# A written-out engine order drawn up anew for the last third of a four-layer kernel, with the residual rows fetched by pairs of tiles

## What is computed

```python
x = x + tanh(g_xattn[0]) * additive_attention(layernorm(x), ctx)            # phase A
x = x + tanh(g_ffn[0]) * quantized_gated_ffn(layernorm(x))                  # phase B, its down projection in C

# third layer, 16 heads of 32 channels, 64 keys per batch
qh = layernorm(x) @ Wq.T + bq
attn = softmax(where(mask, qh @ kh.T / sqrt(32), -inf))
x = x + tanh(g_xattn[1]) * ((attn @ vh) @ Wo.T + bo)

# fourth layer: bit_linear 512 -> 2048, depthwise convolution of 3 taps along the tokens, silu, bit_linear
def bit_linear(x, w):            # 8-bit activations per token, ternary weights
    return act_quant(x) @ weight_quant(w).T
h = bit_linear(layernorm(x), w1)
h = silu(conv_w[0] * h[t-1] + conv_w[1] * h[t] + conv_w[2] * h[t+1] + conv_b)
x = x + tanh(g_ffn[1]) * bit_linear(h, w2)
```

## Time and profile before

| quantity | value |
|---|---|
| median of three runs | 2092.08 us |
| time of the profiled execution | 2092.43 us |
| its span, first to last instruction | 2090.3 us |
| TensorE busy (share of the span) | 1651.5 us (79%) |
| VectorE busy | 1729.7 us (83%) |
| ScalarE busy | 1476.9 us (71%) |
| GpSimd busy | 626.2 us (30%) |
| mean of what DMA moved | 69 GB/s |

### The profile page before, as it was taken

The page is one execution under the profiler, slowest core; times in us unless marked ns, Lnnn a source line. Parts: engine busy times, 40 slices in busy tenths (PEclk is TensorE's granted clock), DMA queues, the critical chain, the costliest instruction groups (busy, mean ns, idle before and its releaser), DMA issues.

```text
span 2090.3 us, 24728 instructions
## 1 busy us (share of the span) xinstructions
PE 1651.5 (79%) x9617; PEld 748.7 (36%) x9686; DVE 1729.7 (83%) x2574; ACT 1476.9 (71%) x1109; POOL 626.2 (30%) x487
## 2 busy tenths in 40 slices
PE   6868866796569767955979678988888888888886
PEld 3212211221113112312434356656666543334332
DVE  6889998999999988885877657877787669999994
ACT  4899999999999999993537434444444466666650
POOL 0000000000000000000612345655555447677773
PEclk9999999999999999997999899999999999999997
DMA  5001100020000100003957423323322112111111
GB/s 189 1 21 46 41 6 1 21 81 11 1 1 16 56 1 1 8 3 112 331 201 263 157 78 94 99 71 101 102 84 86 41 36 66 61 51 51 61 41 61
DMA packets 104551, 143.68 MB, mean 69 GB/s; under 512 B 8046, under 2 KB 61422, under 8 KB 104050
## 3 DMA queue, kind: packets, MB, share of 16 engines
q1 hardware_dynamic: 104434, 142.09, 20.4%
HBM read 91.74 MB, written 50.33 MB: 68 GB/s over the span
## 4 chain that ended last, share of the span: by engine, by line
ACT 41%; PE 32%; DVE 17%; issue 4%; POOL 3%; DMA 2%; SPq 0%; DVEq 0%; POOLq 0%; ACTq 0%
ACT unit L514 37%; PE psum L1598 5%; PE psum L1632 5%; PE psum L1584 4%; DVE hmax_parts L1404 3%; PE psum L1009 3%; PE psum L1015 2%; POOL hidden L1776 2%; DVE psum L1395 2%; DVE unit L423 2%; PE psum L1608 2%; PE psum L1625 2%; DMA xblk<-xnT_scratch 2%; PE psum L1617 1%; DVE hidden_q L1431 1%
## 5 line engine op out<-in xcount | busy, mean ns | idle before, releaser
L514 ACT ACTIVATE unit<-unit 128x4096 f32<-128x4096 f32 x244 | 857.5, 3617 | 0.5 <-DVE unit L423 0.3
L423 DVE TENSOR_SCALAR unit<-feat_proj,text_proj 128x1024 f32<-128x1024 f32 x976 | 667.5, 747 | 67.0 <-PE psum L639 65.3
L639 PE MATMUL psum<-unit,w_pad 128*32 128x512 f32 x3904 | 474.5, 604 | 234.1 <-ACT unit L514 234.1
L639 PEld LDWEIGHTS psum<-unit,w_pad 128*32 128x32 f32 x3904 | 102.6, 109 | 556.8 <-ACT unit L514 398.6
L680 POOL TENSOR_SCALAR red<-red 128x8 f32<-128x8 f32 x4 | 2.0, 510 | 531.5 <-DVE red L321 531.5
L1759 POOL TENSOR_TENSOR h<-h,arow 128x512 f32<-128x512 f32 x104 | 122.3, 1187 | 87.1 <-ACT h L1540 87.1
L1656 PE MATMUL psum<-xq_block,w_q 128*128 128x512 bf16 x489 | 128.1, 399 | 24.5 <-ACT hidden L1563 23.2
L1690 PE MATMUL psum<-w_q,hidden_q 128*128 128x512 fp8e4 x512 | 122.3, 394 | 25.9 <-DVE hidden_q L1431 25.5
L1776 POOL TENSOR_TENSOR hidden<-hidden,srow 128x2048 f32<-128x2048 f32 x32 | 130.5, 4078 | 37.2 <-DVE hidden_q L1431 23.4
L1598 PE MATMUL psum<-xnT_c,wq_sb 128*128 128x256 f32 x512 | 119.9, 388 | 11.0 <-ACT xnT_c L1497 11.0
L547 PE MATMUL psum<-xnT,W_sb 128*128 128x512 f32 x256 | 125.2, 617 | 2.1 <-ACT xnT L465 2.1
(11 more groups left out here) (241 smaller groups left out, 2864.9 us busy)
## 6 DMA issues: line engine op xcount, KB each, us to landing
h_scratch<-h SPq DMA_DIRECT2D x44, 512.0 KB, 3.9
hin<-h_scratch SPq DMA_DIRECT2D x32, 704.0 KB, 5.4
xin<-in_x SPq DMA_DIRECT2D x8, 1024.0 KB, 6.7
tern_in<-in_w1T SPq DMA_DIRECT2D x16, 512.0 KB, 5.6
tern_in<-in_w2T SPq DMA_DIRECT2D x16, 512.0 KB, 5.5
x<-in_x SPq DMA_DIRECT2D x32, 256.0 KB, 2.8
x_scratch<-x SPq DMA_DIRECT2D x32, 256.0 KB, 2.1
x3in<-x_scratch SPq DMA_DIRECT2D x31, 256.0 KB, 2.9
```

Of the source, the lines that this page charges most:

```text
L423: ins = ve.tensor_scalar(units[:, n % 3, k, :], FP[:, bi % 2, k, :], TP[:, k, n:n + 1], None, ALU.add)
L514: ac.activation(units[:, n % 3], units[:, n % 3], ACT.Tanh).then_inc(unit_tanh, 1)
L639: mm = te.matmul(psum[k * TG:(k + 1) * TG, 3 + 2 * grp + half, :], w_pad[:, k, TG - 1 - tt:2 * TG - 1 - tt], units[:, n % 3, k, half * BAN ...
```

## The change

The tables of slots are new in both halves. The period of a group goes from 256 to 226 slots, that of a block from 350 to 363. A tile is further from its first to its last step: the last step of group 0 (XQ) had slot 1084 and has 1276. One convolution chunk moves from TensorE's taps to VectorE's, and one from the multiplication by ScalarE and GpSimd to VectorE's. The residual rows are fetched once per group (512 KB in one transfer, into both tiles of the ring) instead of once per tile, at a slot behind the start of the group and no longer 74 slots ahead of it; the fetch of `hin` moves from HQ1's slots to HQ2's. The arithmetic of each tile stays as it was.

```diff
-    N1, N2, OFF2 = 256, 350, 4330
+    N1, N2, OFF2 = 226, 363, 4140
...
-    DOWN = (38, 102)
+    DOWN = (350, 416)
...
-    X2LOAD = (-74, -50)
-    GP_MID, VE_MID = (0, 1, 2, 4, 5, 6, 7, 9, 10, 11, 12, 13, 15), (3, 8, 14)
-    PE_TAPS, VE_TAPS = (1, 6, 11), (0, 2, 3, 4, 5, 7, 8, 9, 10, 12, 13, 14, 15)
+    X2LOAD = (324,)
+    GP_MID, VE_MID = (0, 1, 2, 3, 5, 6, 8, 9, 10, 12, 13, 15), (4, 7, 11, 14)
+    PE_TAPS, VE_TAPS = (2, 9), (0, 1, 3, 4, 5, 6, 7, 8, 10, 11, 12, 13, 14, 15)
...
             for g, i, t in at1(q, X1):
-                A.wait_ge(x2_loaded[g % GR], 16 * TPG * (g // GR + 1))
+                A.wait_ge(x2_loaded[g % GR], 16 * (g // GR + 1))
...
-        def load_x(t):
-            S.wait_ge(ln3_done, t - X2R + 1)
-            S.wait_ge(x3_stored[t // TPG % GR], 16 * TPG * (t // X2R))
-            sp.dma_start(x2[:, t % X2R, :], x[t * P:(t + 1) * P, :]).then_inc(x2_loaded[t // TPG % GR], 16)
+        def load_x(g):
+            S.wait_ge(ln3_done, TPG * (g + 1 - GR))
+            S.wait_ge(x3_stored[g % GR], 16 * TPG * (g // GR))
+            rows = x[g * GRP:(g + 1) * GRP, :].rearrange("(i p) d -> p i d", p=P)
+            sp.dma_start(x2[:, g % GR * TPG:(g % GR + 1) * TPG, :], rows).then_inc(x2_loaded[g % GR], 16)
 
         def attention(q):
-            for g, i, t in at1(q, HQ1):
+            for g, i, t in at1(q, X2LOAD):
+                load_x(g)
+            for g, i, t in at1(q, HQ2):
                 if t + 2 < NT:
                     load_tile(t + 2)
-            for g, i, t in at1(q, X2LOAD):
-                load_x(t)
...
-        for q in range(X2LOAD[0], QEND):
+        for q in range(min(0, X2LOAD[0]), QEND):
```

More of the change, by code:

```diff
@@ L1235, in flamingo @@
-    PTAP = (239, 316, 416)
-    SILU = (268, 274, 281, 300, 320, 328, 345, 356, 371, 431, 443, 448, 466, 478, 519, 531)
-    AROWMM = (0,)
[L1238 to L1250, removed]
+    N1, N2, OFF2 = 226, 363, 4140
+    LEN1, LEN2 = 1283, 1020
@@ new lines, in flamingo @@
+    SHIFT = (0, 128)
+    HQ1 = (154, 264)
+    HQ2 = (174, 276)
+    DOWN = (350, 416)
+    DSC = (374, 470)
+    X1 = (388, 402)
+    X2ADD = (396, 490)
+    ST2 = (442, 510)
+    ROOT2 = (466, 518)
+    LN2 = (482, 532)
+    BO = (502, 540)
+    TURN2 = (560, 636)
+    XNT = (574, 644)
+    QMM = (668, 740)
+    QT = (700, 772)
+    SCORE = (792, 824)
+    MADD = (802, 840)
+    SMAX = (814, 858)
+    SUB = (826, 870)
+    EXP = (844, 888)
+    SSUM = (874, 900)
+    SREC = (890, 914)
+    NRM = (900, 924)
@@ new lines, in flamingo @@
+    TURNP = (924, 994)
+    PT = (940, 1006)
+    PV = (1002, 1110)
+    OT = (1020, 1122)
+    WO = (1058, 1156)
+    X3 = (1094, 1192)
+    ST3 = (1108, 1200)
+    ROOT3 = (1118, 1208)
+    LN3 = (1134, 1218)
+    AMAX = (1142, 1224)
+    Q3 = (1152, 1230)
+    Y3 = (1158, 1238)
+    TURN3 = (1186, 1270)
+    XQ = (1192, 1276)
+    X2LOAD = (324,)
+    GP_MID, VE_MID = (0, 1, 2, 3, 5, 6, 8, 9, 10, 12, 13, 15), (4, 7, 11, 14)
+    PE_TAPS, VE_TAPS = (2, 9), (0, 1, 3, 4, 5, 6, 7, 8, 10, 11, 12, 13, 14, 15)
@@ new lines, in flamingo @@
+    W1 = (197, 206, 216, 253, 283, 293, 321, 331, 353, 375, 385, 400, 410, 503, 513, 523)
+    VMID = (319, 345, 448, 540)
+    GMID = (213, 229, 240, 269, 309, 339, 390, 401, 411, 454, 522, 565)
+    RAW = (206, 222, 234, 263, 303, 332, 384, 389, 398, 420, 516, 532)
+    TAP0 = (227, 246, 281, 326, 337, 356, 362, 408, 425, 455, 466, 537, 549, 579)
+    TAPS = (239, 301, 332, 350, 362, 375, 387, 472, 484, 497, 528, 546, 558, 589)
+    PTAP = (260, 447)
+    SILU = (253, 315, 320, 346, 369, 379, 393, 403, 486, 491, 498, 511, 544, 560, 574, 603)
@@ L1252, in hit @@
+    AC_ROUND, VE_ROUND = (), (0, 1, 2, 3)
+    HRA = ()
+    HRB = ()
+    HROUND = (762, 822, 872, 933)
+    AROWMM = (0,)
+    AROW = (11,)
+    EDGE = (464, 613)
+    HMAX = (412, 614)
+    HM2 = (656,)
+    HMAXT = (665,)
+    SRED = (676,)
+    S3 = (687,)
+    SROWMM = (701,)
+    SROW = (714,)
+    HS = (720, 784, 836, 895)
+    W2 = (780, 836, 893, 949)
+    OUT = (816, 885, 946, 1012)
     def hit(q, slots, period, count):
```

24 lines of the change are left out of this document (removed).

## The result

| | before | after |
|---|---|---|
| median | 2092.56 us (4 runs, 2088.76 to 2093.64) | 2038.24 us (4 runs, 2033.84 to 2040.56) |
| profiled execution, its span | 2092.43, 2090.3 us | 2038.41, 2036.4 us |

The ratio is 0.9741, with a 95% interval of 0.972 to 0.9762. The prediction was 2055, with a range of 2038 to 2076: the sign and the main mechanism came out, and the time lies 0.2 us above the range's low end. The change gained 54 us where 37 were forecast.

What follows compares the result with a forecast made beforehand. TensorE was taken to bound the attention half and VectorE the convolution half. Attention -44, start -3, join +2 and convolution +8 sum to -37 us, from 2092 to 2055 us, range 2038 to 2076.

Steps and rivals of the forecast that it cites:

- Attention, steady groups: Attention half: TensorE's waits of 3.38 us per group fall to 0.2 over 14 groups, -44 us.
- Rival A: Attention half: handoffs moved, not removed; VectorE late, TensorE waits 1.5 us per group; 2073 us, chance 0.13.
- The start: Start of phase C: first TURN2 waits some 4 us longer for x rows, but later stalls go; -3 us.
- The join: Between attention and convolution halves: a WO moves behind the last SCORE, and the chain there is not filled; +2 us.
- The convolution half: Seven convolution blocks: VectorE gains a tap pair and a VMID, so each block takes 46.2 us, +1.15; +8 us.
- VectorE's work alone is about 42.5 us: Convolution half: VectorE's work per block before the change, from 45.03 us per block and 2.55 us idle.
- I keep the mean of the roundings: Convolution half: each HROUND on VectorE stays at its old mean, 1.99 us, in the new order.
- Rival E: Convolution half reaches its planned 43.2 us per block; 2034 us, chance 0.03.
- Rival B: Convolution half loses more: each rounding at 2.28 us, idle time kept, +23 in place of +8; 2070 us, chance 0.06.
- the rule on VectorE and GpSimd: Convolution half: a 2-port VectorE tensor_scalar and a GpSimd instruction exclude each other; without it, 16 us lower.
- Rivals C and D: C: ring of eight x tiles delays fetches, 2123 us, chance 0.05. D: order immaterial in time, 2092 us, chance 0.03.

Runs made afterwards that it cites:

- the first profile: Profiled execution of the changed kernel as first measured, nothing else altered; 2038.41 us, span 2036.4 us, median 2038.24 us.
- The fetch alone: Changed kernel with x of group 0 fetched ahead of the third and fourth hin transfer, other groups unaltered; 2034.55 us.
- fetch and X1 together: Changed kernel with x of group 0 fetched earlier and ScalarE's X1 of group 0 put ahead of the SHIFTs of group 1; 2030.23 us.
- the second profile: Changed kernel run again unaltered, beside the version that fetches x by tile; median 2036.06 us.
- The moved steps: Kernel before the change, with only HM2 (slot 593 to 616) and S3 (647 to 634) moved; 2084.31 us.
- the one chunk: Kernel before the change, with tap chunk 11 done by ScalarE and VectorE instead of TensorE; 2096.68 us.
- one of 0.69 put back: Changed kernel with the first half of QMM directly behind TURN2 again (slot 640 for 668); 2056.82 us.
- The third profile above: Changed kernel run once more unaltered, beside the version with x of group 0 and X1 moved earlier; median 2032.05 us.

## Why the prediction was right and where it failed

*Attention, steady groups* (-44, bounds -47 and -26): right in mechanism and nearly in size. A group without waits was read as 26.9 us before the change and measured as 26.90 after it. The 0.2 us left per group did not appear: all 3.36 us went, which gives 14 x 3.36 = 47, the good bound. From the mark at 1250 us (the second SCORE of the second group, at 1245.41 after) to the last SCORE the stretch went from 418.0 to 372.8 us, -45, where the forecast and the moved WO make -47. Rival A (waits come back since VectorE runs late) fell: VectorE is busy 25.05 of 26.9 us, 93% and not the 84% of the working, because its fast steps meet more GpSimd instructions (HQ1 took 1.96 and 2.13 us in that group, 1.87 and 0.88 in the earlier trace rows; LN3 1.18 and 1.49, where it took 0.54 before), and yet nothing on TensorE waits in the steady groups.

*The start* (-3, bounds +6 and -8): from the first DOWN to the mark at 1250 us it was 65.0 us and is 59.3 up to the same SCORE, -5.7, inside the bounds. TURN2 waits 4.7 us longer in the first profile, as expected, but for another cause: what holds it up is X1's place in ScalarE's queue, and not the fetch. The fetch alone changed nothing; fetch and X1 together brought TURN2 3 us and the first SCORE 5 us forward.

*The join* (+2): with the WO that moved 3.4 us across the mark, +5.6 measured against +5.4 expected.

*The convolution half* (+8, bounds -3 and +23): this is the step that failed. The result, -9, lies outside its bounds. Two sentences carried the error. "VectorE's work alone is about 42.5 us" took durations lengthened beside GpSimd instructions for durations of the work, in HM2 and S3 above all, which the rows read did not list. "I keep the mean of the roundings" took a property of the old order for one of the instruction. The prediction also calls the rounding of 1.41 us in the earlier trace rows one that ran alone; a GMID from 1837.76 to 1839.04 us ran beside its start, and alone the rounding takes 1.22 us, as in the changed kernel at 1758.81. By the rows of four blocks before and after, per block: HM2 1.33 to 0.68, -0.65; the tensor_scalars of S3 0.61 and 0.74 to 0.16 and 0.20, -0.99; roundings 4 x (1.99 - 1.77), -0.88; together -2.5 us. VectorE's busy time shows the sum: 42.4 us + 2.05 - 2.5 = 41.95, and four blocks of the changed kernel have 167.84 / 4 = 41.96. The idle time fell from 2.55 to 1.9 us, about as assumed (1.65). The block was forecast at 46.2 us and took 43.7, and 7 x 2.5 = 17 us is the whole miss. Blocks at a granted clock of 1.00 take 42.7; in the second profile, where six of the seven do, the seven blocks gained 17 us instead of 9.

That the time still fell inside the range is luck, in two ways. The range's low end was 2038, said to be half the way from 2055 to 2030, but half the way is 2042.5; and the medians of the same kernel in the two repetitions, 2036.06 and 2032.05 us, lie below 2038.

The moved steps (-7 us with no instruction less) show that such meetings set the time; the one chunk (+0.7 instead of +1.44) shows that the price of a step depends on what it pushes apart. Rival E, the plan's 43.2 us, was given 0.03 because "VectorE's work is 44.55"; with 43.7 us per block it is the rival that came true for this half, its sign (HM2 to HM2 below 44.5) was seen, and its 2034 us are nearer to the result than the forecast. It had been dismissed by the same mistake. Rival B, a block above 47 us, did not come.

In this half the prediction applied the rule on VectorE and GpSimd to the four roundings alone. HM2 took 1.33 us beside a GMID and 0.68 without. What the Trainium skill says (SBUF — State Buffer, Who interferes with whom) of tensor_scalars in a 2-port mode it also says of a VectorE instruction with two SBUF inputs beside a GpSimd one that reads SBUF; HM2 is such a tensor_tensor, and the trace agrees.

*Rivals C and D*: the ring of x tiles never held anything up, since the group ran at TensorE's 26.9 us, and the order was not immaterial.

## What to carry to other kernels

A duration in a profile is one of the instruction in its company. Before adding a VectorE step to a sum, compare its shortest and its mean duration, and look at what GpSimd did beside the long ones; a new order changes that share, and in this kernel it was worth more than the work that was moved. On an engine that is busy all the time, every handoff that the order leaves back to back costs its wait in each round: 3.38 us of waits taken out shortened the group by 3.36, and one of 0.69 put back lengthened it by 0.91. Putting another independent step between cost nothing here.

## What was not expected of the hardware

A GpSimd-VectorE meeting costs small steps most in proportion: a tensor_scalar of 128 x 4 elements took 0.92 us beside a GMID and 0.20 without.

A block of the convolution half takes 42.7 us when TensorE's granted clock is 1.00 in it, and 44.2 to 45.6 when it is 0.96 to 0.93, although VectorE is the busiest engine in it. The third profile above shows both kinds one behind the other. In the second profile of the changed kernel every block but the last ran at 1.00, the span was 2029.7 us, and seven blocks took 298.4 us in place of 306.0. The slow block of the first profile (1776.20 to 1821.80 us) runs in two places at the lower of the two levels for a time. The first two rows are these places, and the third is the second of them in the profile without slow blocks:

```profile
1779.05 3.29 PE L1659 MATMUL psum<-xq_block,w_q 128*128 128x512 bf16 x8 [1.46 <-ACT hidden L1566]
...
1798.84 5.32 PE L1693 MATMUL psum<-w_q,hidden_q 128*128 128x512 fp8e4 x16 [2.15 <-DVE hidden_q L1434]
```

```profile
1796.07 3.63 PE L1693 MATMUL psum<-w_q,hidden_q 128*128 128x512 fp8e4 x16 [1.74 <-DVE hidden_q L1434]
```

From 1778 to 1783 and from 1799 to 1804 us the granted clock is 0.66, and the two rows take 1.4 and 1.7 us more than in the other profile (1.90 and 3.63). The block is 2.9 us longer, so hardly anything of TensorE's delay is hidden behind VectorE. TensorE had waited ahead of both, but it waits at the same places when the clock stays at 1.00 (1.46 and 1.74 us), so the waits alone do not explain the fall.

The slow blocks are always the same ones. In all seven other profiles with this order of the convolution half (the first and third of the changed kernel and those of five experiments) the distances between HM2 are 42.7 us for the second and the fourth, 45.6 for the third, 44.2 for the fifth, and 44.2 or 42.7 for the sixth. The kernel before had a block at 0.96 too, but it cost it less (45.4 against 45.1 us). Why one execution has none of them stays open. It is 7.6 us between the first two profiles, out of the spread of 2028 to 2041 us that the changed kernel shows.
